# Four streams of eight attention layers on one core: the steps of every engine in a new order

## The chip, the core and the metric

One core of a Trainium2 chip runs the whole program. Its engines each work through a queue of their own: TensorE (PE; its weight loads are shown apart as PEld), VectorE (DVE), ScalarE (ACT), GpSimd (POOL) and SyncE (SP), which here issues the DMAs. The metric is the device time of the program in microseconds, as a median of several runs. "Span" is the time from the first to the last instruction of one profiled execution.

## What is computed

64 sequences of 64 tokens with 128 features, and as many of context, go through eight attentions and what stands between them (layer norms, feed-forward blocks, residual sums). The reference, cut to one attention and to what sets the shapes:

```python
x   = normal((64, 64, 128))          # the sequences
ctx = normal((64, 64, 128))          # their context

def attention(q_in, kv_in, Wq, Wk, Wv, heads, key_mask, query_mask, causal):
    Q, K, V = split(q_in @ Wq), split(kv_in @ Wk), split(kv_in @ Wv)
    scores = Q @ K.T / sqrt(dk)      # 64 x 64 for each sequence and head
    scores = where(key_mask, -inf, scores); if causal: scores = where(col > row, -inf, scores)
    return softmax(scores) @ V * query_mask
# layer 0: two attentions of 16 heads, with layer norms and fc1, fc2
# layer 1: one of 16 heads, output projection, feed-forward of 512 with a gate
# layer 2: two of 16 heads (one causal), output projections, feed-forward of 512 with relu
# layer 3: three times: relu on Q, K, V, 4 heads, layer norm by the sample's deviation, leaky block
```

Attentions 0 to 4 have 16 heads (8 pairs), attentions 5 to 7 have 4 heads (2 pairs).

## The kernel before

**Tiling.** Eight sequences form a stream, four streams form a group, and two groups (0 and 1) cover the 64 sequences. A stream's tensors lie as 128 partitions x 512 elements. Every piece of work is a step with a name, and it belongs to a group, an attention (0 to 8, where 8 is the tail behind attention 7) and a stream (0 to 3). `1.4.2` in the tables is group 1, attention 4, stream 2.

**What sets the order.** Nothing is scheduled when the program is built. The dictionary `ORDER` holds a hand-over list for each engine, `walk` reads it, and `step` issues the instructions of one name. Each step waits on semaphores for its operands, and on PE also for the readers of the PSUM bank that it writes. Every engine works strictly through its list, so a step that waits holds up all that is behind it. PSUM has eight banks in four pairs (`pair0` to `pair3`).

**The names on PE.** `x`, `x1`, `q`, `kv`, `o`, `ctx` are transposes of 128x512 (L695). `pq`, `pk`, `up0` to `up3` are single projections (L708); `pv` writes V in 64x64 pieces (L815); `wo`, `fc2` are L702, `down` L782, `ff` L792. `first`, `length`, `ksum`, `maskrow` make the key mask (L826 to L846). Scores are made twice: `A0`, `A1` (bf16, L916, mask terms L911) only to find each row's maximum, and `B0`, `B1` (f32, the same lines), which are exponentiated. `maxrow` (L846) turns the maxima into a row that B adds. `v0` to `v3` multiply probabilities by V (L935; L964 for 4 heads), and `t0`, `t1` turn the result back (L949).

**The names elsewhere.** DVE reduces A (`mx0` to `mx3`, L1363), negates (`nm`, L1343), spreads the rows (`mrow`, `lrow`, L1350), scales the outputs (`O0`, `O1`, L1153 and L1164), and does sums, layer norm statistics (`sum`, `kvstats`, `n3q`: L1085, L1088) and norms (`n1`, `n3`: L1108; `nq`, `nkv`: L1095). ACT exponentiates B (`e0` to `e3`, L1011) and moves PSUM to SBUF (L977). POOL makes reciprocal deviations and some sums.

**Filling requests.** On PE, `name@24` says which banks a step takes, and `+3` behind it asks for three filling requests ahead of it: products of a constant bf16 tile (`warm`, L683) into the banks that the step is about to write. They compute nothing. A request is one product of 128x512, or four or two side by side on parts of the array. The list before has 323 requests at 244 steps, 581 matmuls in all.

**SP.** Its later loads and stores stand in three loops: the four `Xin` of group 1, the four `C` of group 1, the outputs of group 0, then those of group 1.

Of the kernel before, what the change touches and what calls it, by code (L numbers as in the profile page):

```python
# [32 lines left out]
STREAMS = 4  # L33
# [24 lines left out]
        v2@1+1 v3 t1@5; 0.0.3 maskrow@7; 0.0.1 B0@01 B1@20+1; 0.0.2 A1@12+2; 0.0.1 v0@6+1 v1 v2@3+2 v3 t0@6 t1@3+3;
        0.0.2 maxrow@7+2; 0.0.3 A0@02+3; 0.0.2 B0@31+1; 0.1.0 x1@1+1 kv@0; 0.0.3 A1@31; 0.1.0 pk@1+1 pq@0; 0.0.2 B1@23
        v0@1; 0.1.0 first@0+1; 0.1.1 x1@7; 0.0.2 v1; 0.0.3 maxrow@6; 0.0.2 v2@5 v3 t0@4 t1@5; 0.0.3 B0@13+1 B1@02;  # L60
        0.1.0 pv@3 length@2+1; 0.1.1 kv@7; 0.0.3 v0@6+1; 0.1.2 x1@7+1; 0.1.1 pk@2; 0.1.0 maskrow@5; 0.1.1 pq@4; 0.0.3
        v1; 0.1.0 A0@01+1; 0.0.3 t0@6; 0.1.2 kv@7+1; 0.0.3 v2@5 v3; 0.1.0 A1@01; 0.0.3 t1@5; 0.1.2 pk@7+1; 0.1.1
        first@6 pv@7+2; 0.1.2 pq@6; 0.1.0 maxrow@5; 0.1.1 length@4+3; 0.1.0 B0@01+1 B1@23; 0.1.1 maskrow@1; 0.1.2
        first@0; 0.1.0 v0@1; 0.1.1 A0@12; 0.1.0 v1; 0.1.3 x1@0; 0.1.0 t0@1+1; 0.1.3 kv@0+1; 0.1.1 A1@13; 0.1.2 pv@5
        length@4; 0.1.0 v2@1 v3; 0.1.3 pk@0; 0.1.2 maskrow@4; 0.1.1 maxrow@1+3; 0.1.2 A0@13+1; 0.1.3 pq@5+2; 0.1.0
        t1@4; 0.1.1 B0@01+1; 0.1.3 first@7 pv@6+2; 0.1.2 A1@01+1; 0.1.3 length@7; 0.2.0 kv@6; 0.1.1 B1@20 v0@6 v1;
        0.1.3 maskrow@7; 0.1.2 maxrow@5+1; 0.2.0 pk@4; 0.1.1 v2@5; 0.1.3 A0@01; 0.1.1 t0@7+1 v3; 0.2.0 pv@6; 0.1.1
# [1431 lines left out]
```

## Time and profile before

| | us |
|---|---|
| median of three runs | 1085.9 |
| lowest, highest | 1084.7, 1085.9 |
| span of the profiled execution | 1085.1 |
| of it PE busy, of that filling | 1005.6, 113.4 |
| DVE busy | 840.9 |
| ACT busy | 635.8 |
| POOL busy | 320.4 |

The device time of the profiled execution itself is not among the numbers; the three runs lie 0.4 us below to 0.8 us above its span, so the span stands for it.

A busy share here is a union: two instructions of one engine that overlap count once, so groups of lines add up to more than the engine's busy time. A matmul's duration holds its way through the array, and the next one starts earlier than the last one ends. How long a step holds PE is therefore read from start to start in the timeline.

### The profile page before, as it was taken

The page shows a single profiled execution, that of the slowest core. Times are in us where ns is not written, and L with a number is a line of the kernel's source. Part 1 is how long each engine was busy: PE and PEld are TensorE (multiplying, and loading weights), DVE is VectorE, ACT ScalarE, POOL GpSimd, SP SyncE. Part 2 cuts the span into 40 slices and gives each one's busy share as a digit, 9 for nine tenths or more (in the row PEclk, how much of TensorE's full clock was granted, in tenths as well). Part 3 has the DMA queues.
Part 4 walks back from the last instruction along what each step waited for, and adds up shares of the span by engine and source line. Part 5 has one row for each costly group of instructions (what it writes and reads, how often), then busy time and mean ns, then how long its engine had stood idle before and what let it go on. Part 6 is the DMA issues. An engine that isn't in the chain of part 4 may idle for free.

```text
span 1085.1 us, 38818 instructions
## 1 busy us (share of the span) xinstructions
PE 1005.6 (93%) x16923; PEld 725.6 (67%) x16957; DVE 840.9 (77%) x2336; ACT 635.8 (59%) x938; POOL 320.4 (30%) x405
## 2 busy tenths in 40 slices
PE   8889988899999999999999998889999999998996
PEld 5657665576777677767776776556767677677674
DVE  5897999867476756789878899999567774679986
ACT  5346565567777464555645655556777766464652
POOL 4022245511000113346450313553011020336531
PEclk9999999999999999999979999999999999999998
DMA  7000000000000000000010000000000000000001
GB/s 255 3 22 23 2 3 3 2 2 2 3 3 3 12 9 14 11 2 2 2 31 2 3 13 3 2 2 2 3 2 3 3 3 3 1 2 2 2 2 40
DMA packets 13722, 13.60 MB, mean 13 GB/s; under 512 B 617, under 2 KB 13170, under 8 KB 13298
## 3 DMA queue, kind: packets, MB, share of 16 engines
q1 hardware_dynamic: 13554, 11.11, 3.2%
q8 instruction: 136, 2.23, 0.9%
q14 instruction: 32, 0.26, 0.1%
HBM read 9.01 MB, written 2.10 MB: 10 GB/s over the span
## 4 chain that ended last, share of the span: by engine, by line
PE 42%; DVE 28%; ACT 5%; issue 3%; POOL 2%; POOLq 0%; DVEq 0%; ACTq 0%
PE pair L708 8%; DVE mx L1363 7%; PE pair L916 7%; PE pair L911 5%; PE pair L782 4%; PE pair L695 4%; PE pair L935 3%; DVE stats L1085 3%; PE pair L815 2%; DVE Y L1164 2%; ACT PT L1011 2%; PE pair L702 2%; PE pair L683 2%; DVE Y L1108 2%; PE pair L949 2%
## 5 line engine op out<-in xcount | busy, mean ns | idle before, releaser
L1011 ACT ACTIVATE PT<-pair 128x1024 f32<-128x1024 f32 x184 | 180.3, 1029 | 124.8 <-PE pair L916 115.7
L1363 DVE TENSOR_REDUCE mx<-pair 128x16 f32<-128x1024 f32 x184 | 218.4, 1215 | 42.1 <-PE pair L916 41.6
L916 PEld LDWEIGHTS pair<-KQ 32*128 32x128 f32 (+3 forms) x4416 | 170.7, 157 | 37.6 <-DVE mx L1363 3.4
L916 PE MATMUL pair<-KQ 32*128 32x128 f32 (+3 forms) x4416 | 180.0, 254 | 2.4 <-DVE mx L1363 1.0
L708 PE MATMUL pair<-xf,W_all 128*128 128x512 f32 x336 | 177.4, 623 | 3.2 <-ACT xf L977 1.0
L1390 POOL TENSOR_SCALAR ve<-mv 128x4 f32<-128x4 f32 x64 | 17.0, 265 | 503.3 <-DVE mv L1088 432.5
L683 PE MATMUL pair<-warm 128*128 128x512 bf16 (+3 forms) x581 | 113.4, 395 | 17.8 <-DVE Y L1164 7.8
L977 ACT ACTIVATE KQ<-pair,c 128x512 f32<-128x512 f32 x160 | 100.3, 692 | 42.9 <-PE pair L708 42.2
L935 PE MATMUL pair<-PT,V 128*32 128x64 f32 x5120 | 94.2, 221 | 2.2 <-ACT PT L1011 0.7
L977 ACT ACTIVATE V<-pair 64x512 f32<-64x512 f32 x128 | 79.1, 618 | 26.5 <-PE pair L815 24.7
L935 PEld LDWEIGHTS pair<-PT,V 128*32 128x32 f32 x5120 | 78.3, 110 | 22.2 <-issue 8.7
L708 PEld LDWEIGHTS pair<-xf,W_all 128*128 128x128 f32 x336 | 54.9, 191 | 34.5 <-issue 14.7
L977 ACT ACTIVATE xf<-pair 128x512 f32<-128x512 f32 x80 | 47.4, 598 | 50.6 <-PE pair L695 50.0
L977 ACT ACTIVATE T<-pair 128x512 f32<-128x512 f32 x80 | 48.1, 603 | 42.8 <-PE pair L935 42.5
L1085 DVE BATCH_NORM_STATS2 stats<-X 128x6 f32<-128x128 f32 x320 | 69.8, 281 | 3.7 <-POOL X L1414 1.1
L683 PEld LDWEIGHTS pair<-warm 128*128 128x128 bf16 (+3 forms) x581 | 29.1, 97 | 62.4 <-DVE Y L1164 11.5
L1392 POOL TENSOR_TENSOR rstd<-ve,expo 128x4 f32<-128x4 f32 x64 | 66.6, 1041 | 5.3
L1108 DVE SCALAR_TENSOR_TENSOR Y<-X,mv,row 128x128 f32<-128x128 f32 x192 | 60.8, 378 | 0.9
L977 ACT ACTIVATE KQ<-pair,cols 128x512 f32<-128x512 f32 x72 | 49.5, 696 | 19.5 <-PE pair L708 19.5
L782 PE MATMUL pair<-W_all,KQ 128*128 128x128 f32 x512 | 60.5, 277 | 0.3 <-DVE KQ L1308 0.2
L782 PEld LDWEIGHTS pair<-W_all,KQ 128*128 128x128 f32 x512 | 58.5, 192 | 1.4 <-ACT KQ L977 0.6
L1153 DVE RECIPROCAL rd<-pair 128x32 f32<-128x32 f32 (+1 forms) x128 | 37.4, 292 | 26.3 <-PE pair L949 19.6
(122 smaller groups left out, 1824.0 us busy)
## 6 DMA issues: line engine op xcount, KB each, us to landing
W_all<-weights SPq DMA_DIRECT2D x1, 2880.0 KB, 13.7
Xin<-x SPq DMA_DIRECT2D x8, 256.0 KB, 3.6
C<-ctx SPq DMA_DIRECT2D x8, 256.0 KB, 4.1
out<-X SPq DMA_DIRECT2D x8, 256.0 KB, 2.5
row<-rows SPq DMA_DIRECT2D x1, 1024.0 KB, 6.1
c<-const SPq DMA_DIRECT2D x1, 504.0 KB, 5.5
W_all<-weights SPq DMA_DIRECT2D x1, 192.0 KB, 2.9
c<-const SPq DMA_DIRECT2D x1, 80.5 KB, 2.0
```

What stands on the lines that cost most here:

```text
L683: pe.matmul(bank[c, at:at + FILL], warm[r, 0:columns_], warm[r, :].unsqueeze(1).broadcast_to((rows_, FILL // 128, 128)), start=True, stop= ...
L708: pe.matmul(t[:, 0:TOK], W(name), src[:], start=True, stop=True).then_inc(*banks.full(*use))
L782: mm = pe.matmul(t[:, 128 * j:128 * j + 128], hid[s][:, c, 128 * j:128 * j + 128], W(f"d{a - 1}_{c}"), start=c == 0, stop=c == 3)
L911: pe.matmul(banked[u // 2][:, at:at + 512], fixed, spread, start=u not in begun, stop=False, skip_group_check=True)
L916: last[u] = pe.matmul(banked[u // 2][:, at:at + 2 * S], stationary[rows_, seq].rearrange("p r t -> p (r t)"), moving[rows_, seq].rearrange ...
L935: mm = pe.matmul(outputs[s][32 * c:32 * c + WIDE, at:at + S], V8_padded[s][:, first:first + WIDE], p[:, c // 2, b, c % 2, :], start=True, ...
L977: act.activation(dst, src, f, **kw).then_inc(*banks.drain(use, operand, *event))
L1011: act.activation(PT[:, place, :], banks.of("B", a, s, v)[:], ACT.Exp, scale=float((D // (2 * PAIRS[a])) ** -0.5)).then_inc(*banks.drain((" ...
L1085: dve.bn_stats(stats[lane(tag)][:, j, :], src[:, j, :]).then_inc(*vec.mark("stats", *tag))
L1108: dve.scalar_tensor_tensor(out=Y[s][:, j, :], in0=X[s][:, j, :], scalar=mv[i][:, j, 0:1], in1=rowb(name + "_g"), op0=ALU.subtract, op1=ALU ...
L1363: dve.tensor_reduce(dst, banks.of("A", a, s, v)[:].rearrange("p (u m t) -> p u m t", u=2, t=S), AX.X, ALU.max).then_inc(*banks.drain(("A", ...
L1392: g_.tensor_tensor(rstd[i][:], ve[i][:], expo[:, 0, :], ALU.pow).then_inc(*pool.mark("rstd", *tag))
```

## The change

The lists of PE, ACT, DVE and POOL are replaced by others. They hold the same steps, as many as before: 1152 on PE, 776 on ACT, 849 on DVE, 176 on POOL. What differs is the order, the banks that PE's steps take, the slots of the probabilities, and the filling requests: 148 at 57 steps, 226 matmuls. Streams 2 and 3 stand further behind streams 0 and 1 than before. Steps of attention 5 that depend only on the context (`ksum`, `pv`, `maskrow`, and `km`, `lrow` on DVE) and the transposes `ctx` now stand in the stretch of attentions 1 and 2. SP's later loads and stores get a list too; it names the same sixteen in the same order. `outputs` gets a key for each half, since `v2` may now stand ahead of the use of the first half.

The diff, of the tables only their first lines:

```diff
 ORDER = {
     "PE": """
-        0.0.0 x@7+1; 0.0.1 x@6; 0.0.0 pq@7 pk@6; 0.0.3 x@5; 0.0.1 pq@4+1; 0.0.2 x@7; 0.0.1 pk@3 pv@2+1; 0.0.0 pv@6
-        first@7; 0.0.2 pq@3; 0.0.0 length@7; 0.0.3 pq@6+1; 0.0.0 maskrow@7+2; 0.0.3 pk@2; 0.0.0 A0@02; 0.0.1
...
+        pq@3; 0.0.0 maskrow@0; 0.0.3 x@1; 0.0.2 pv@2; 0.0.0 A0@23; 0.0.2 pq@0; 0.0.1 pk@1; 0.0.0 A1@12; 0.0.3 pq@0;
...
+    "SP": """
+        1.0.0 xin; 1.0.1 xin; 1.0.2 xin; 1.0.3 xin; 1.0.0 cin; 1.0.1 cin; 1.0.2 cin; 1.0.3 cin; 0.8.0 out; 0.8.1 out;
+        0.8.2 out; 0.8.3 out; 1.8.0 out; 1.8.1 out; 1.8.2 out; 1.8.3 out
     """,
...
-                for section.group in range(1, GROUPS):
-                    for s in range(STREAMS):
+                def step(name, a, s):
+                    if name == "xin":
                         sp.wait_ge(*vec.at("sum", 1, s, ago=1))
                         sp.dma_start(Xin[s][:], x_g[section.group, s]).then_inc(*x_in[s].mark(by=16))
-                    for s in range(STREAMS):
+                    elif name == "cin":
                         sp.wait_ge(*banks.ready("pk", 5, s, ago=1))
                         sp.wait_ge(*banks.ready("pv", 5, s, ago=1))
                         sp.dma_start(C[s][:], c_g[section.group, s]).then_inc(*c_in[s].mark(by=16))
-                for section.group in range(GROUPS):
-                    for s in range(STREAMS):
+                    elif name == "out":
                         sp.wait_ge(*(vec if section.group == GROUPS - 1 else pool).at("enc", 8, s))
                         sp.dma_start(o_g[section.group, s], X[s][:]).then_inc(*x_out[s].mark(by=16))
+
+                walk("SP", step)
...
-                        outputs[s] = room("OT", a, s, v // 2)
+                        outputs[s, v // 2] = room("OT", a, s, v // 2)
```

On PE, in group 0 between attentions 1 and 2. `X3`, `Y3` and the like are the tiles of stream 3; `warm` rows are filling requests. Before:

```order
L683 MATMUL pair0<-warm 128x512
L695 MATMUL pair0<-c32,X3 128x128 x4
L683 MATMUL pair0<-warm 128x512
L702 MATMUL pair0<-W_all,kf0 128x128 x4
L683 MATMUL pair0<-warm 128x512
L708 MATMUL pair0<-xf3,W_all 128x512
L683 MATMUL pair3<-warm 128x512
L846 MATMUL pair3<-c16,nm81 128x64
L683 MATMUL pair3<-warm 128x512 x3
L695 MATMUL pair3<-c32,C0 128x128 x4
```

After, in the same stretch (L707 is what L695 was, L720 what L708 was, L961 what L949 was, L858 what L846 was, L850 what L838 was, L822 and L827 what L810 and L815 were):

```order
L961 MATMUL pair3<-c32,T20 128x128 x4
L707 MATMUL pair3<-c32,Y21 128x128 x4
L707 MATMUL pair0<-c32,Y20 128x128 x4
L707 MATMUL pair0<-c32,C1 128x128 x4
L707 MATMUL pair3<-c32,C0 128x128 x4
L850 MATMUL pair1<-kz1,c16 128x8
L850 MATMUL pair1<-kz0,c16 128x8
L720 MATMUL pair0<-kf0,W_all 128x512
L827 MATMUL pair3<-W_all,kf0 64x64 x16
L707 MATMUL pair0<-c32,Y22 128x128 x4
L858 MATMUL pair2<-c16,nm81 128x64
```

The filling has gone from between the steps, and the transposes of the context (`C0`, `C1`) with attention 5's key sums (`kz0`, `kz1`) have come forward.

On DVE, attention 5's mask work (`lm2`, `lrow`, `kms`). Before, it stands in attention 5 of its stream, among the reductions of attention 4:

```order
L1128 TENSOR_REDUCE am0<-X0 128x4
L1131 TENSOR_SCALAR qm0<-am0 128x4
L1363 TENSOR_REDUCE mx3<-pair1 128x2x8
L1363 TENSOR_REDUCE mx3<-pair0 128x2x8
L1363 TENSOR_REDUCE mx3<-pair2 128x2x8
L1335 TENSOR_SCALAR lm20<-pair1 64x8x2 x2
L1343 TENSOR_SCALAR nm83<-mx3 64x64 x2
L1350 TENSOR_TENSOR lrow0<-pair0,c32 32x512
L1355 TENSOR_TENSOR kms0<-pair0,c32 32x128
```

After, it stands in attention 2 (L1347 is what L1335 was, L1375 what L1363 was):

```order
L1120 SCALAR_TENSOR_TENSOR Y1<-X1,mv1,row 128x128 x4
L1347 TENSOR_SCALAR lm20<-pair1 64x8x2 x2
L1347 TENSOR_SCALAR lm21<-pair1 64x8x2 x2
L1347 TENSOR_SCALAR lm23<-pair3 64x8x2 x2
L1347 TENSOR_SCALAR lm22<-pair2 64x8x2 x2
L1375 TENSOR_REDUCE mx3<-pair0 128x2x8
L1375 TENSOR_REDUCE mx3<-pair1 128x2x8
L1097 BN_STATS stats1<-X1 128x6 x4
L1100 BN_AGGR mv1<-stats1 128x2 x4
L1362 TENSOR_TENSOR lrow1<-pair3,c32 32x512
L1367 TENSOR_TENSOR kms1<-pair3,c32 32x128
L1362 TENSOR_TENSOR lrow0<-pair3,c32 32x512
```

All four streams' mask work is now done there, ahead of attention 3.

## Rows read from the trace of the kernel before

**Rows 1.** The page's part on busy time (us, share of the span, instructions).

```profile
span 1085.1 us, 38818 instructions
PE 1005.6 (93%) x16923; PEld 725.6 (67%) x16957; DVE 840.9 (77%) x2336; ACT 635.8 (59%) x938; POOL 320.4 (30%) x405
```

**Rows 2.** Seven stretches: length, each engine's busy time, granted clock, DMA share, GB/s.

```profile
27.00:217.00 190.00, 167.73 (x3448) 116.96 (x3444) 169.04 (x493) 102.27 (x145) 59.28 (x68) 0.97 0.03 8
217.00:461.00 244.00, 237.13 (x3933) 172.71 (x3940) 161.87 (x410) 155.04 (x229) 44.23 (x53) 1.00 0.02 7
461.00:650.00 189.00, 181.31 (x2877) 133.50 (x2889) 158.42 (x443) 106.45 (x160) 72.07 (x80) 0.96 0.03 8
650.00:759.00 109.00, 95.69 (x1735) 65.57 (x1730) 104.34 (x319) 62.94 (x92) 49.31 (x56) 1.00 0.01 2
759.00:1030.00 271.00, 258.51 (x4284) 191.15 (x4295) 192.12 (x519) 172.99 (x256) 66.40 (x80) 1.00 0.01 2
```

**Rows 3.** The same stretches for L683 alone, the filling (PE, PEld busy).

```profile
27.00:217.00 190.00, 35.54 (x203) 8.96 (x203) 0.97 0.03 8
217.00:461.00 244.00, 18.61 (x84) 4.77 (x84) 1.00 0.02 7
650.00:759.00 109.00, 21.63 (x128) 5.80 (x128) 1.00 0.01 2
```

**Rows 4.** Timeline of PE: start, us, line, tiles, count.

```profile
229.33 1.06 PE L916 MATMUL pair<-KQ 32*128 32x128 f32 x32
230.22 0.39 PE L911 MATMUL pair<-mrow,c 32*128 32x512 bf16 x4
...
231.72 0.40 PE L683 MATMUL pair<-warm 128*32 128x512 bf16 x4
231.94 0.62 PE L935 MATMUL pair<-PT,V 128*32 128x64 f32 x32
...
233.46 0.38 PE L683 MATMUL pair<-warm 128*128 128x512 bf16 x1
233.67 1.02 PE L708 MATMUL pair<-xf,W_all 128*128 128x512 f32 x2
```

**Rows 5.** DVE's costliest groups by shape: busy, mean ns of one, idle before.

```profile
L1363 DVE TENSOR_REDUCE mx<-pair 128x16 f32<-128x1024 f32 x184 | 218.4, 1215 | 42.1 <-PE pair L916 41.6
L1085 DVE BATCH_NORM_STATS2 stats<-X 128x6 f32<-128x128 f32 x320 | 69.8, 281 | 3.7 <-POOL X L1414 1.1
L1108 DVE SCALAR_TENSOR_TENSOR Y<-X,mv,row 128x128 f32<-128x128 f32 x192 | 60.8, 378 | 0.9
```

**Rows 6.** Who PE waited for: us in total, times, longest.

```profile
PE pair L683 <- DVE Y L1164: 7.8, 7, 2.9
PE pair L846 <- DVE nm L1343: 6.6, 9, 2.1
PE pair L911 <- DVE mrow L1350: 5.3, 7, 1.7
PE pair L949 <- ACT T L977: 4.1, 10, 0.8
...
PE pair L911 <- DVE mx L1363: 1.3, 5, 0.3
```

**Rows 7.** Short stretches around two falls of the granted clock.

```profile
45.00:48.00 3.00, 0.94 (x21) 0.56 (x9) 2.62 (x6) 0.60 (x1) 0.00 (x0) 1.00 0.04 8
48.00:51.00 3.00, 2.67 (x36) 1.79 (x40) 2.86 (x14) 0.00 (x0) 0.00 (x0) 0.51 0.00 0
...
548.00:551.00 3.00, 1.48 (x7) 0.61 (x9) 2.57 (x5) 1.75 (x4) 2.27 (x2) 0.81 0.00 0
554.00:557.00 3.00, 3.00 (x16) 2.91 (x14) 1.94 (x6) 1.66 (x3) 2.69 (x4) 0.50 0.00 0
```

**Rows 8.** Whom SP waited for.

```profile
SPq L658 <- PE pair L815: 332.4, 4, 272.0
```

**Rows 9.** The whole core: span and mean granted clock.

```profile
core 0: 1085.1 us, clock 0.986
```

More of the change, by code:

```diff
@@ L58 @@
[L58 to L67, printed above, removed]
@@ L168 @@
[L168 to L172 removed]
+        0.0.0 x@0; 0.0.1 x@1+6; 0.0.0 pq@0 pk@1 pv@2; 0.0.1 pv@0; 0.0.0 first@1+2; 0.0.2 x@2; 0.0.0 length@1; 0.0.1
@@ new lines @@
+        ctx@1; 0.3.0 ctx@7; 0.5.1 ksum@2; 0.5.0 ksum@3; 0.2.0 pk@0 pv@7; 0.1.2 kv@1; 0.1.1 maxrow@4; 0.5.1 pv@5; 0.5.0
+        pv@0; 0.1.2 pk@1 pv@4 first@1; 0.1.1 B0@23; 0.1.3 x1@0 kv@4; 0.1.1 v0@5 v1; 0.1.2 length@1; 0.1.3 pk@4 pv@5;
+        0.2.0 x1@0; 0.1.2 maskrow@4; 0.1.1 B1@30 t0@5; 0.1.2 A0@02; 0.1.1 v2@6 v3; 0.2.1 pk@7; 0.1.1 t1@6; 0.1.2
+        A1@20; 0.2.1 pv@7; 0.1.3 pq@6; 0.2.0 fc1@0; 0.2.2 kv@1; 0.3.2 ctx@7; 0.1.2 maxrow@4; 0.5.2 ksum@5; 0.5.3
+        ksum@6; 0.2.0 fc2@0; 0.5.2 pv@1+1; 0.1.3 first@7; 0.2.1 x1@1+2 fc1@1; 0.1.3 length@0; 0.2.1 fc2@7+3; 0.1.3
@@ new lines @@
+        maskrow@3+2; 1.0.3 A0@03; 1.1.1 pk@2; 1.0.3 A1@23; 1.1.0 A0@13; 1.1.1 pv@4 first@5; 1.0.2 B1@13 v0@0; 1.0.3
+        maxrow@1; 1.1.1 length@4; 1.0.2 v1; 1.1.0 A1@32; 1.0.2 t0@0; 1.1.1 maskrow@1; 1.0.2 v2@2 v3; 1.2.0 kv@0; 1.0.2
+        t1@2; 1.3.0 ctx@3; 1.0.3 B0@23; 1.5.0 pv@0; 1.1.1 A0@13; 1.1.0 maxrow@1; 1.0.3 v0@4 v1; 1.5.0 ksum@5; 1.0.3
+        B1@13 t0@4; 1.1.0 B0@03; 1.0.3 v2@2 v3; 1.1.0 v0@4+1 B1@01; 1.0.3 t1@6; 1.1.0 v1; 1.1.2 kv@7 x1@2; 1.2.0 pk@3;
+        1.1.2 pq@4; 1.1.0 t0@6 v2@2 v3; 1.1.2 pk@7 pv@2; 1.1.0 t1@4; 1.1.1 A1@03; 1.1.2 first@4; 1.1.3 x1@2; 1.2.1
@@ new lines @@
+        kv@3; 1.2.0 pv@0; 1.1.1 maxrow@1; 1.1.3 pq@2; 1.3.1 ctx@3; 1.1.1 B0@30; 1.1.2 length@4; 1.1.3 kv@2; 1.1.1
+        v0@6; 1.1.2 maskrow@4; 1.1.1 v1; 1.1.3 pk@2; 1.1.1 B1@03 t0@3; 1.1.3 first@4; 1.2.1 pk@2; 1.1.1 v2@0 v3; 1.1.3
+        length@1 pv@4; 1.1.2 A0@13; 1.1.3 maskrow@5; 1.1.1 t1@0; 1.2.0 x1@4; 1.2.2 kv@1; 1.2.0 fc1@4; 1.1.2 A1@13;
+        1.2.1 pv@0; 1.2.0 fc2@1; 1.3.2 ctx@4; 1.2.3 kv@0; 1.3.3 ctx@4; 1.5.1 ksum@6; 1.5.0 maskrow@7; 1.5.2 pv@0;
+        1.5.3 pv@4; 1.5.1 pv@0; 1.1.3 A0@12; 1.1.2 maxrow@0; 1.2.1 x1@1 fc1@1; 1.1.3 A1@21; 1.2.1 fc2@1; 1.5.2 ksum@0;
@@ L173 @@
+        1.7.1 B0@2; 1.7.2 ksum@1 x@2 maskrow@3+1; 1.7.1 v0@0+1 v1@1; 1.7.2 pq@2 pk@0; 1.7.3 ksum@3 x@4; 1.7.2 pv@5
+        A0@0; 1.7.3 pq@2 pk@3 maskrow@0; 1.7.2 maxrow@1; 1.7.3 pv@4; 1.7.2 B0@3; 1.7.3 A0@0; 1.8.1 x1@2; 1.7.2 v0@3
+        v1@4; 1.8.1 ff@2; 1.7.3 maxrow@5 B0@0+3 v0@3+5 v1@0; 1.8.2 x1@0+6 ff@0; 1.8.3 x1@1+2 ff@1
     """,
     "ACT": """
[L175 to L176 removed]
```

508 lines of the change are left out of this document (254 added, 254 removed).

## The prediction

> **What bounds the kernel now.** I read the busy shares first, then busy time by stretches, then the filling alone, then the timeline of PE. PE is busy for 1005.6 of 1085.1 us and DVE for 840.9 [rows 1], but 113.4 us of PE is filling (the table above), so its own work is 892 us. The stretches show two regimes. In 217 to 461 us PE is busy for 237.1 of 244 us, with 18.6 of filling, while DVE is busy for 161.9: PE bounds [rows 2, 3]. In 27 to 217 us (attentions 0 to 2 of group 0) DVE is busy for 169.0 of 190 us, and in 650 to 759 us, the same place in group 1, for 104.3 of 109; there PE's own work is 167.7 - 35.5 = 132.2 and 95.7 - 21.6 = 74.1 us [rows 2, 3]. DVE bounds there, and PE waits or fills. 461 to 650 and 759 to 1030 us are mixed, PE ahead.
>
> How long a step holds PE is read from start to start. A half of the f32 scores with its row terms holds it for some 1.2 us (0.89 from 229.33 to 230.22, and the row terms ahead of it), and one filling request for 0.22 us: 231.72 to 231.94 for four products side by side, 233.46 to 233.67 for one wide one [rows 4]. So the 323 requests hold PE for 323 x 0.22 = 71 us, less than the 113.4 us of their durations.
>
> **Fewer requests.** 148 are left, 33 us; 175 x 0.22 = 38.5 us of PE time goes. Whether it comes back depends on the bound. I cut PE's list into twenty parts of equal own work (867 us by start to start, 43.4 each; part 0 is the first) and counted. Parts 1 to 3 and 11 to 13, the DVE-bound ones, had 161 requests and have 37. Parts 4 to 10 and 14 to 18, where PE bounds, had 102 and have 59. The first and the last part had 60 and have 52. In the DVE-bound parts the 124 that go (27 us) turn into waiting, since what is late there is DVE. In the PE-bound parts the 43 that go, 9.5 us, come back where the operand was there anyway. In 217 to 461 us PE was idle for only 6.9 us [rows 2], so it seldom still waited behind its filling. I take 8 us, with bounds of 0 and 38.5.
>
> **The balance of DVE against PE.** A step of one engine costs the same wherever it stands; what changes is which steps share a stretch. For each part I added the DVE durations that become due in it (10 to 14 reductions `mx` in each of parts 1 to 3 and 11 to 13 at 1.215, statistics at 0.281, norms at 0.378 [rows 5], and the rest alike). Added singly they come to 961 us, where the busy union is 840.9, so I scale by 0.875. The heaviest parts fall: part 2 from 65 to 59 us, part 12 from 70 to 56. Their neighbours rise: part 1 from 47 to 52, part 3 from 43 to 51, part 13 from 37 to 51. Taking in each part the longer of PE, DVE and ACT, the twenty sum to 948 us before and 938 after: 10 us less, nearly all in group 1. So the further lag of streams 2 and 3 evens a peak but does not turn DVE-bound parts into PE-bound ones. The sum explains 948 of 1085 us; the other 137 are filling on the path and waits within the parts. Bounds: 0 (DVE was not the last in the peak) and 15.
>
> **Distances between a step and what it waits for.** In PE's list I measured the own work between a producer and its consumer, to see where a wait becomes shorter. Longer at the lower quarter or median: `v3` to `t1` from 0.5 to 1.2 us, `pq` to `A0` from 4.2 to 5.7 (median), `A1` to `maxrow` from 3.3 to 4.0, `wo` to the next `q` from 6.6 to 7.8 (median). Shorter: `B0` to `v0` from 2.9 to 2.1 (median), `x1` to `ff` from 1.0 to 0.6, `length` to `maskrow` from 2.3 to 1.1 (median). The waits that the longer ones touch are `maxrow` for `nm`, 6.6 us, the row terms for `mrow`, 5.3, and `t` for ACT, 4.1 [rows 6]. I take 6 us off; bounds are 16 off (all three) and 6 on.
>
> **Banks.** The new list takes banks back sooner. Between the step that fills a score bank and the one that takes it next, the lower quarter of the 368 `mx` cases had 2.3 us of PE work and has 1.8; over all steps, cases under 1.5 us rise from 309 to 382. A reader like `mx` needs 1.215 us [rows 5] once the bank is full, and PE's queue stands still meanwhile with all four streams behind it. Waits of this kind show little before: 1.3 us for `mx` at L911 [rows 6], but 7.8 us of waits for the outputs `Y` stand ahead of filling, which takes its step's bank. I take 4 us on: of the 73 new short cases, those outside the DVE-bound parts, about 40, at 0.1 us each. Bounds are 0 and 73 x 0.5 = 36.
>
> **Edits at nothing.** SP's list names the same sixteen transfers in the same order, and SP spends hundreds of microseconds waiting, 332.4 us at one line [rows 8]; that slack covers them. The moved `pv`, `ctx` and `ksum` of attention 5 are eight sets of about 1.3 + 0.5 + 0.1 us on PE, 15 us that go from PE-bound parts to parts where PE has room; their `km` and `lrow` on DVE (about 1.3 us a stream) go the wrong way. Both are in the part sums. `C` is free for group 1's load no later than before, as `pk` of attention 5, which stays, releases it.
>
> **Clock.** The mean granted clock is 0.986 [rows 9]. It fell from 2.4 to 1.2 GHz behind 3 us in which PE was busy for 0.94 us, and again behind 1.48 of 3 [rows 7]. Without filling PE would be busy for 132 of 190 us in the first DVE-bound stretch, far above those two cases on average, but waits will be longer in places. I take 0 and bound it at 15 us, which is a doubling of the some 30 us at the lower level ((1 - 0.986) x 2 x 1085) at half their length each.
> The Trainium skill (TensorE: Matmul & The Clock Gate, "The HAM clock gate") says that the throttled clock is the default and that sustained activity releases it, which speaks against taking filling out. The falls in the trace agree, and by that rule some of the 38.5 us would be given back, which is the third rival below.
>
> **The sum.** -8 (requests) -10 (balance) -6 (distances) +4 (banks) = -20 us. The span of 1085.1 stands 0.8 us under the median of 1085.9, so the forecast is **1066 us**, 1.8% less.
>
> **Rivals.** First, much faster: the lists fit so well that filling in the DVE-bound parts was itself on the path, as a late PE step makes DVE late. For it: DVE was still idle for 21 of 190 us there [rows 2]. Then 27 us of requests come back too, and the distances give their 16: 1085.9 - 8 - 27 - 10 - 16 + 4 = 1029 us.
> Second, slower: banks decide. If the 73 new short reuses each cost the 0.5 us by which one falls short of `mx`, the sum is -24 + 36 = +12 us, **1098 us**. It beats the gains from about 50 such waits on. For it: one queue, eight banks, and more own work in each microsecond. Against it: before, PE stood idle for 79 us in all, and most reuses stood well clear of their readers.
> Third, no change: the clock. PE idles longer in the DVE-bound parts, the falls double (+15 us) and the banks cost a little more: about 1084 us.
>
> **How the numbers follow.** Chances: forecast (1050 to 1081) 0.42, much faster 0.20, no change 0.10, slower 0.28, the last above the evidence for banks alone since 1152 steps in a new order leave room for waits that distances do not show. A comparison can tell about 0.2%, 2 us, from nothing. Faster is 0.42 + 0.20 = 0.62, same 0.10, slower 0.28. The range reaches from 1033 us, just above the first rival, to 1102, beyond the second, and leaves out about a tenth on each side.
>
> **What would show it.** The filling busy time should fall from 113.4 to about 52 us (226 matmuls). In the PE-bound stretches PE should stay over 95% busy with hardly any filling, and both should be shorter than now. In attentions 0 to 2 DVE should be 90% busy or more and PE idle should grow. If banks decide, `mx` and the outputs `Y` lead the waits of PE, at far more than 8 us. If the clock decides, the mean granted clock is under 0.97. The prediction is wrong at its root if the DVE-bound stretches shorten by more than 20 us, or if PE idles for over 10% in attentions 3 and 4.

## The result, and the profile after

The changed kernel takes 1098.28 us (median of 7 runs, 1089.12 to 1100.13) against 1085.9 (7 runs): ratio 1.0098, 95% interval 1.0080 to 1.0116. It is 12.4 us slower by the medians (10.6 by the ratio, which goes by means), where 20 us less was forecast. The profiled execution of after has a span of 1097.4 us. Its part on busy time:

```profile
span 1097.4 us, 38302 instructions
PE 987.4 (90%) x16602; PEld 717.4 (65%) x16602; DVE 855.7 (78%) x2336; ACT 643.7 (59%) x938; POOL 321.0 (29%) x405
```

Against [rows 1], PE is busy for 18.2 us less (1005.6 before), but the span is 12.3 us longer: idle PE time grew from 79.5 to 110.0 us. DVE is busy for 14.8 us more with the same 2336 instructions. The stretches of [rows 2], in the same columns:

```profile
27.00:217.00 190.00, 162.31 (x3389) 116.62 (x3388) 165.83 (x476) 105.91 (x152) 53.16 (x61) 0.95 0.03 8
217.00:461.00 244.00, 230.30 (x3793) 169.00 (x3794) 173.81 (x432) 157.45 (x229) 54.11 (x64) 0.98 0.02 7
461.00:650.00 189.00, 176.05 (x2843) 128.30 (x2841) 159.00 (x457) 105.14 (x155) 69.95 (x81) 0.97 0.03 8
650.00:759.00 109.00, 89.42 (x1710) 66.35 (x1710) 93.85 (x274) 63.23 (x93) 41.32 (x46) 0.92 0.01 2
759.00:1030.00 271.00, 258.70 (x4154) 189.14 (x4155) 195.43 (x515) 173.94 (x254) 66.93 (x78) 1.00 0.01 2
```

and the filling alone (L695 now) in two of them, as [rows 3]:

```profile
27.00:217.00 190.00, 9.00 (x45) 2.39 (x45) 0.95 0.03 8
650.00:759.00 109.00, 1.21 (x4) 0.31 (x4) 0.92 0.01 2
```

Two things are to be seen. DVE doesn't fill the stretches that it was to bound: 165.8 of 190 us and 93.9 of 109, where it had 104.3 of 109 before. And the granted clock (the column behind the busy times) is lower in three of the five: 0.95, 0.98 and 0.92 where before has 0.97, 1.00 and 1.00. (The same stretch of time does not hold quite the same steps in both.) Over the whole core it is 0.968 against 0.986 [rows 9]. PE's waits, as [rows 6] (us in total, times, longest); the row left out is the wait for the first loads:

```profile
PE pair L923 <- DVE mx L1375: 10.1, 11, 1.6
PE pair L923 <- ACT PT L1023: 9.4, 14, 2.1
PE pair L707 <- DVE Y L1107: 6.2, 4, 2.5
PE pair L707 <- DVE X L1127: 4.9, 2, 2.8
PE pair L720 <- ACT xf L989: 4.8, 8, 1.0
...
PE pair L695 <- DVE Y L1176: 3.1, 3, 1.3
PE pair L923 <- DVE Y L1176: 3.0, 2, 2.7
PE pair L928 <- DVE mx L1375: 3.0, 4, 2.0
PE pair L923 <- DVE mrow L1362: 2.8, 5, 0.9
```

L923 writes the row terms, the first products into a score bank; `mx` (DVE) and `PT` (ACT) are the readers of the score banks. These two are waits for a bank, and neither led before. Summed over all rows of that view, from before to after: `nm`, `mrow` and `T`, the operands that the new distances were to help, fall from 7.0 + 7.2 + 4.8 to 1.1 + 3.2 + 2.2 us, 12.5 less. `mx` and `PT` rise from 4.6 + 5.9 to 15.1 + 17.0, 21.6 more (of the waits for `PT`, 1.5 and 2.7 us are those of `v` for its operand, not for a bank). `Y`, `X` and `xf` rise from 13.1 + 2.2 + 1.0 to 18.6 + 6.0 + 7.1, 15.4 more. Within `Y` it is the norm (L1107, before L1095) that rises, from 2.6 to 7.7; the attention's outputs `Y` (L1176, before L1164) stay at 10.3 and 9.9. So these 15.4 us are mostly ends of normalisation chains and the moves `xf` to SBUF, not banks. (A wait for several semaphores stands under the last.)

### The profile page after: what moved, and what is told of

The parts are those of the page before. It is cut to its first block, busy times and chain, and to the rows that moved or that the text cites. A ratio compares the mean times of both kernels' runs of the same rounds, so it can differ in the third digit from the quotient of the medians.

```text
span 1097.4 us, 38302 instructions
## 1 busy us (share of the span) xinstructions
PE 987.4 (90%) x16602; PEld 717.4 (65%) x16602; DVE 855.7 (78%) x2336; ACT 643.7 (59%) x938; POOL 321.0 (29%) x405
## 4 chain that ended last, share of the span: by engine, by line
PE 64%; DVE 27%; ACT 4%; issue 3%; POOL 1%; DMA 0%; SPq 0%; POOLq 0%; ACTq 0%; DVEq 0%
PE pair L720 13%; PE pair L928 11%; PE pair L923 8%; PE pair L947 7%; DVE mx L1375 6%; PE pair L707 5%; PE pair L794 5%; PE pair L827 3%; PE pair L961 3%; DVE stats L1097 2%; PE pair L714 2%; ACT PT L1023 2%; PE pair L838 2%; DVE rq L1169 2%; DVE Y L1176 2%
## 5 line engine op out<-in xcount | busy, mean ns | idle before, releaser
L1023 ACT ACTIVATE PT<-pair 128x1024 f32<-128x1024 f32 x184 | 182.9, 1023 | 160.5 <-PE pair L928 152.5
L1375 DVE TENSOR_REDUCE mx<-pair 128x16 f32<-128x1024 f32 x184 | 219.9, 1218 | 45.4 <-PE pair L928 44.0
L928 PEld LDWEIGHTS pair<-KQ 32*128 32x128 f32 (+3 forms) x4416 | 175.5, 163 | 42.0 <-issue 6.7
L928 PE MATMUL pair<-KQ 32*128 32x128 f32 (+3 forms) x4416 | 185.4, 260 | 5.4 <-DVE mx L1375 3.0
L720 PE MATMUL pair<-xf,W_all 128*128 128x512 f32 x336 | 174.8, 625 | 5.6 <-ACT xf L989 4.8
L1402 POOL TENSOR_SCALAR ve<-mv 128x4 f32<-128x4 f32 x64 | 16.9, 264 | 471.4 <-DVE mv L1100 471.4
L947 PEld LDWEIGHTS pair<-PT,V 128*32 128x32 f32 x5120 | 78.5, 111 | 28.4 <-issue 16.2
L720 PEld LDWEIGHTS pair<-xf,W_all 128*128 128x128 f32 x336 | 54.3, 191 | 39.3 <-issue 17.9
L923 PE MATMUL pair<-mrow,c 32*128 32x512 bf16 (+1 forms) x368 | 47.1, 395 | 25.0 <-ACT PT L1023 9.2
L1362 DVE TENSOR_TENSOR mrow<-pair,c 128x512 bf16<-128x512 f32 (+1 forms) x64 | 43.6, 682 | 20.5 <-PE pair L858 20.1
L1299 DVE SCALAR_TENSOR_TENSOR X<-pair,X 128x512 f32<-128x512 f32 x40 | 27.5, 688 | 39.7 <-PE pair L714 21.3
```

What stands on the lines that cost most here:

```text
L720: pe.matmul(t[:, 0:TOK], W(name), src[:], start=True, stop=True).then_inc(*banks.full(*use))
L923: pe.matmul(banked[u // 2][:, at:at + 512], fixed, spread, start=u not in begun, stop=False, skip_group_check=True)
L928: last[u] = pe.matmul(banked[u // 2][:, at:at + 2 * S], stationary[rows_, seq].rearrange("p r t -> p (r t)"), moving[rows_, seq].rearrange ...
L947: mm = pe.matmul(outputs[s, v // 2][32 * c:32 * c + WIDE, at:at + S], V8_padded[s][:, first:first + WIDE], p[:, c // 2, b, c % 2, :], star ...
L1023: act.activation(PT[:, place, :], banks.of("B", a, s, v)[:], ACT.Exp, scale=float((D // (2 * PAIRS[a])) ** -0.5)).then_inc(*banks.drain((" ...
L1362: dve.tensor_tensor(dst[s][0:n, :].rearrange("p (m t) -> p m t", m=8), banks.of(*use)[0:n, 0:S].unsqueeze(1).broadcast_to((n, 8, S)), K32( ...
```

## The experiments

All were timed beside before on the same chip; ratios are to before there (medians 1081.25 to 1087.15 us), with 95% intervals. "Part n" is a twentieth of PE's own work, as in the prediction.

### Order and filling apart

e1: the new order with the old 323 requests at the steps where the old list has them. e2: the old order with the new 148 at their 57 steps. e3 and e4: either order with none. Only the +n in PE's list change; e2 and e3 begin:

```
-        0.0.0 x@7+1; 0.0.1 x@6; 0.0.0 pq@7 pk@6; 0.0.3 x@5; 0.0.1 pq@4+1; ...
+        0.0.0 x@7; 0.0.1 x@6+6; 0.0.0 pq@7 pk@6; 0.0.3 x@5; 0.0.1 pq@4; ...      (e2)
+        0.0.0 x@7; 0.0.1 x@6; 0.0.0 pq@7 pk@6; 0.0.3 x@5; 0.0.1 pq@4; ...        (e3)
```

> The new order with the filling requests of the old one: the same 323 at the same 244 steps, in place of its own 148. Theory CLOCK (the 12 us come from the filling that went, by way of the granted clock and of waits that it had covered): the mean granted clock returns to about 0.985 and the time falls to 1080 to 1088 us. Rival ORDER (the new order waits more in itself): the clock returns too, but the time stays at 1094 us or more, since 175 requests more are 38 us of work on PE and only part of them falls into waits.

Measured: 1131.84 us, 1.0461 (1.0438 to 1.0485).

> The old order with the new filling: 148 requests at the 57 steps at which the new order has them, the other 175 gone. Theory CLOCK: slower than 1085.9 by about 8 to 15 us, with a mean clock of 0.97 or less. Rival ORDER: 1075 to 1086 us, since requests that delayed ready steps in the parts bound by PE are gone (my prediction's term was 8 us), whatever the clock does.

Measured: 1093.19 us, 1.0104 (1.0083 to 1.0125).

> The old order with no filling request at all. Theory CLOCK: clearly slower, 1100 us or more, with the mean clock under 0.95. Rival ORDER: within 10 us of 1085.9, what the lower clock costs being given back by 71 us of PE time that is no longer taken.

Measured: 1079.27 us, 0.9981 (0.9966 to 0.9997).

> The new order with no filling request. Theory CLOCK: 1105 to 1115 us, clock under 0.955. Rival ORDER: within 4 us of 1098, as its 148 requests stand in few bunches where PE waits anyway.

Measured: 1098.65 us, 1.0159 (1.0134 to 1.0184).

Of the two theories ORDER's times hold for e1, e3 and e4 (though e1's clock came back only to 0.974). In e2 it fails: its 1075 to 1086 us were missed, and the time is 12 us above before's there, as CLOCK had it.

Without any filling the new order is 19.4 us slower, more than the whole loss. By the ratios the loss adds up from the runs alone: taking the old filling away -2 us (1.0000 to 0.9981), the new order in place of the old one +19 (0.9981 to 1.0159), its own filling put in -7 (1.0159 to 1.0098), together +10.6. In the old order all 323 requests, 71 us of holding PE, cost 2 us net. Requests put at the other order's steps cost 14 us (e2 over e3) and 33 us (e1 over e4).

The pages of e3 and e4 (spans 1079.5 and 1096.3 us) show where the new order's loss lies:

```profile
PE 956.1 (89%) x16342; PEld 702.3 (65%) x16376; DVE 839.5 (78%) x2336; ACT 635.3 (59%) x938; POOL 322.1 (30%) x405
```

```profile
PE 954.2 (87%) x16340; PEld 704.1 (64%) x16376; DVE 855.1 (78%) x2336; ACT 644.1 (59%) x938; POOL 321.6 (29%) x405
```

PE is busy for as long in both. What grows is its idle time, from 123.4 to 142.1 us. PE's waits in e3, then e4:

```profile
PE pair L859 <- DVE nm L1356: 16.9, 15, 3.4
PE pair L924 <- DVE mrow L1363: 7.7, 10, 1.4
PE pair L962 <- ACT T L990: 7.0, 15, 1.1
...
PE pair L924 <- ACT PT L1024: 4.6, 6, 1.2
...
PE pair L924 <- DVE mx L1376: 2.7, 7, 1.1
```

```profile
PE pair L724 <- DVE Y L1124: 12.8, 6, 4.1
PE pair L940 <- DVE mx L1392: 9.8, 10, 1.6
PE pair L940 <- ACT PT L1040: 9.8, 15, 2.1
PE pair L724 <- DVE X L1144: 8.0, 2, 5.5
...
PE pair L940 <- DVE mrow L1379: 4.6, 5, 1.8
...
PE pair L875 <- DVE nm L1372: 3.2, 3, 1.7
```

The exchange of before and after shows bare: `nm` falls from 16.9 to 3.2 us at its line, and `mx`, `PT` and the chain ends `Y` (L1124 is the norm) and `X` more than take its place.

### Filling fitted to the waits

e5 and e6 give either order as many requests as fitted into the waits for an operand that e3 and e4 showed: 190 at 76 steps, and 166 at 51. From e4 to e6:

```
-        0.0.0 x@0; 0.0.1 x@1; 0.0.0 pq@0 pk@1 pv@2; 0.0.1 pv@0; 0.0.0 first@1; ...
+        0.0.0 x@0; 0.0.1 x@1; 0.0.0 pq@0 pk@1 pv@2; 0.0.1 pv@0; 0.0.0 first@1+7; ...
```

> The old order with 190 filling requests at 76 steps, each as many as fit into the wait for an operand that the same order showed there without any filling (one request for every 0.27 us of a wait over 0.4 us). CLOCK (the time follows how long the granted clock is low, 56 us of the old order's span without filling and 78 us of the new one's, at about half a microsecond lost for each): the requests lie in idle time and keep the clock up, so the time falls under the 1079.3 us without filling, to about 1065. STRUCTURE (the low clock only goes along with the waits, it doesn't make them): a fitted request saves nothing and costs what it overlaps, 1079 to 1090 us.

Measured: 1084.13 us, 0.9997 (0.9969 to 1.0025).

> The new order with 166 filling requests at 51 steps, fitted in the same way to the waits that the new order showed without filling. CLOCK: low clock falls from 78 us to under 40 and the time from 1098.7 us to about 1078, and the distance to the old order with fitted filling shrinks from 19 us to under 8. STRUCTURE: 1095 to 1105 us, the distance stays 15 us or more, whatever the clock shows.

Measured: 1101.64 us, 1.0156 (1.0119 to 1.0193).

Whole core of e3, then of e5:

```profile
core 0: 1079.5 us, clock 0.971
```

```profile
core 0: 1077.5 us, clock 0.986
```

The clock rose and the time didn't fall, so CLOCK as written (half a microsecond gained for each at the upper level, requests free in the waits) is refuted; both runs lie where STRUCTURE had them, and the orders stay 17 us apart. What CLOCK left out is what the requests hold up; the section on why the prediction was wrong puts both together.

### GpSimd's additions of a bias row

e7 and e8 cut all 68 of GpSimd's additions of a bias row to a 128x512 tile to one element, in the old and the new order. The biases are left out of the result; the expectation calls the rows zeros, which they are not.

```
-                    g_.tensor_tensor(X[s][:], X[s][:], rowb(name + "_b").unsqueeze(1).broadcast_to((P, NT, 128)),
+                    g_.tensor_tensor(X[s][:, 0, 0:1], X[s][:, 0, 0:1], rowb(name + "_b")[:, 0:1],
```

> The old order and its own filling, with GpSimd's 68 additions of a bias row to a whole 128x512 tile (1.27 and 1.36 us each, all the rows are zeros) cut to one element a partition. PORT (VectorE's norms are held while such an addition runs, up to 1.43 us for a norm of 0.34 us): VectorE's busy falls by 10 us or so in both orders, more in the new one. The chain behind each norm gets 1.2 us shorter in both, so this run is only the base for the next: 1065 to 1085 us.

Measured: 1059.72 us, 0.9772 (0.9737 to 0.9807).

> The same cut in the new order with its own filling. PORT: the distance between the orders, 12.4 us with the additions, shrinks to under 5 us, and no norm of VectorE takes over 0.8 us. STRUCTURE or CLOCK: the distance stays 10 us or more, though the long norms are gone.

Measured: 1088.08 us, 1.0025 (0.9999 to 1.0051).

The distance grew to 28.4 us instead of shrinking, so PORT isn't why the new order is slower. (The two runs also lie far apart in clock, which is priced in the section on why the prediction was wrong: PE was at the lower level for 7.4 us in e7 and for 64.3 in e8, means of their runs.) But the cost is real: DVE's busy time falls by 26.1 us in the old order (840.9 to 814.8) and by 23.5 in the new (855.7 to 832.2), though none of its own instructions changed. The page of e7:

```profile
PE 994.6 (94%) x16923; PEld 719.8 (68%) x16957; DVE 814.8 (77%) x2336; ACT 635.7 (60%) x938; POOL 247.6 (23%) x405
```

### Spliced orders

e9 to e14 have no filling. Every engine goes by one order up to a point of time in its trace, and by the other for the steps that are left; e12 changes twice. PE's list at the joint, from e4 to e9:

```
-        1.0.1 length@5; 0.7.3 A0@1; 1.0.1 maskrow@4; 0.7.3 maxrow@5; 1.0.1 A0@01 A1@23; 0.7.3 B0@0; 1.0.0 ...
+        1.0.1 length@5; 0.7.3 A0@1; 1.0.1 maskrow@4; 0.7.3 maxrow@7 B0@0 v0@6 v1@3; 0.8.2 x1@6 ff@2; 1.0.2 x@3 ...
```

> No filling. Every engine goes by the new order up to 552 us of its trace (584 of TensorE's steps, just before the second group's attentions start) and from there by the old one. PLACES (the 19 us by which the new order is slower without filling lie where the per-part comparison of the two traces puts them: nothing net before 552 us, 8 us from there to 760 us, 9 us in the last 60 us): this one costs what the old order costs, 1078 to 1082 us, ratio 0.998 to 1.001. EVERYWHERE (the loss is spread, each stretch under the new order costs its share): 1088 us, ratio 1.007.

Measured: 1092.42 us, 1.0060 (1.0040 to 1.0080).

> No filling. The old order up to 546 us (579 of TensorE's steps), then the new one. PLACES: all of the loss is there, 1095 to 1099 us, ratio 1.013 to 1.016. EVERYWHERE: 1088 us, ratio 1.007. SEED (the new order's later part is only bad because of the state in which its own first part leaves the streams and banks): 1079 to 1083 us here, and 1088 or more in the run before.

Measured: 1117.66 us, 1.0269 (1.0242 to 1.0295).

> No filling. The new order up to 798 us of its trace (847 of TensorE's steps: the second group's attentions 0 to 4 are behind it), then the old one. PLACES: keeps the 8 us lost between 552 and 760 us and saves the 9 us of the last 60 us: 1086 to 1091 us, ratio 1.005 to 1.009. If the last 60 us are slow because streams 2 and 3 stand behind streams 0 and 1 and not because of the steps' order there, the old order can't mend it: 1095 us or more.

Measured: 1098.48 us, 1.0108 (1.0092 to 1.0125).

> No filling. The old order up to 260 us (253 of TensorE's steps), the new one to 552 us, then the old one again. The per-part comparison gives the new order 3 to 6 us in the stretch bound by TensorE (parts 4 to 9). PLACES: 1073 to 1077 us, ratio 0.993 to 0.996, faster than both kernels. EVERYWHERE: 1084 us, ratio 1.003.

Measured: 1100.15 us, 1.0119 (1.0104 to 1.0133).

All four are slower than PLACES had them, by 2 us (e11) to 17 us (e12) over the end of its range, by the ratios. By its total alone e9 would fit EVERYWHERE (1.007), and e11 a tail that is slow by the lag (1095 us or more). The parts of PE's list (us more than in e3; start of the part in e3), worked out from one profiled execution of each, show why:

```
part  from     e4    e9   e10   e11   e12   e13   e14
 0-3     0    2.8   3.8  -2.4  -0.2   2.8  -1.1  -2.1
   4   248   -0.9  -0.5   0.0  -0.5   7.5  -0.5   0.0
 5-9   295   -1.8  -1.8   0.0  -1.8  -1.7  -1.9   0.0
  10   543    5.1  12.9  13.0   5.1  11.3   5.1   1.4
  11   595    4.0   1.3   7.6   7.1   1.3   4.0   0.0
  12   645   -6.4  -0.5  -4.1  -4.0   1.6  -6.4   0.1
  13   712    5.2   1.8   5.6   5.4   0.1   5.2   0.8
14-18   766    0.4   1.3   3.5  11.6  -0.3   3.4   6.3
  19  1012    8.7  -1.1  10.0  -1.3  -1.1  -1.5   8.9
```

Outside a joint a part costs what its order costs in it, whatever stood before: parts 5 to 9 give -1.7 to -1.9 wherever the new order runs there, the last part 9 to 10 us wherever the new order runs and -1.1 to -1.5 wherever the old one does. That is PLACES. (Parts 0 to 3, 11 and 12 differ by 3 to 6 us between traces of one order, so smaller differences say nothing.) What the expectations left out is the joint, 7 to 13 us each (part 10 in e9, e10 and e12; part 4 in e12; parts 14 to 17 in e11): there a few steps, 5 to 12 of PE's in e9 to e11, are done that the other order would have done later, and others are missing. So e13 and e14 change over where only 5 or 6 steps over all engines differ, at 964 and 958 us, and swap the tail alone. From e4 to e13:

```
-        1.5.3 down@2; 1.6.1 x1@3; 1.6.0 pk@0; 1.5.3 x@1; 1.6.1 ff@2; 1.6.0 pq@3; 1.5.2 maxrow@0; 1.6.0 ...
+        1.5.3 down@2; 1.6.1 x1@3; 1.6.0 pk@0; 1.5.3 x@1; 1.6.1 ff@2; 1.5.3 pk@3; 1.6.0 pq@2; 1.6.1 x@5; 1.6.0 ...
```

> No filling. The new order up to 964 us (1036 of TensorE's steps), where both orders have done the same steps but for 5 over all engines, then the old one. PLACES (the last stretch is slow by its own order): the 9 to 11 us of the last 60 us come back and the joint costs under 2 us: 1088 to 1091 us, ratio 1.004 to 1.008, against 1.0159 of the whole new order. LAG (the tail is slow because streams 2 and 3 come to it later): 1096 us or more.

Measured: 1092.37 us, 1.0054 (1.0030 to 1.0077).

> No filling. The old order up to 958 us (1035 of TensorE's steps), then the new one: the mirror of the run before. PLACES: the old order's 1079.3 us and the tail's 9 to 11: 1088 to 1091 us, ratio 1.005 to 1.009. LAG: 1079 to 1082 us.

Measured: 1098.31 us, 1.0115 (1.0084 to 1.0146).

The ratio moves from 1.0159 to 1.0054 with the old tail, and from 0.9981 to 1.0115 with the new one: 11 and 15 us. LAG falls; the tail's own order is slow. (e14 lies 7 us above PLACES' range: beside 8.9 us in the last part it has 6.3 more in parts 14 to 18, around the joint.) PE's timeline at the end (start, us, line, tiles; in brackets the idle time before), e3 then e4:

```profile
1060.94 1.18 PE L977 MATMUL pair<-V,PT 128*64 128x66 f32 x32 [1.11 <-ACT PT L1024]
1062.05 0.66 PE L708 MATMUL pair<-c,X 128*128 128x128 f32 x4
...
1063.68 1.05 PE L805 MATMUL pair<-W_all,xf 128*128 128x128 f32 x8
...
1069.59 1.12 PE L708 MATMUL pair<-c,X 128*128 128x128 f32 x4 [2.33 <-DVE X L1128]
...
1071.80 1.91 PE L805 MATMUL pair<-W_all,xf 128*128 128x128 f32 x8
```

```profile
1039.24 0.66 PE L724 MATMUL pair<-c,X 128*128 128x128 f32 x4 [2.84 <-POOL X L1443]
...
1047.17 1.41 PE L724 MATMUL pair<-c,X 128*128 128x128 f32 x8 [2.51 <-DVE X L1144]
...
1076.78 1.15 PE L993 MATMUL pair<-V,PT 128*64 128x66 f32 x32 [1.11 <-ACT PT L1040]
1083.45 1.12 PE L724 MATMUL pair<-c,X 128*128 128x128 f32 x4 [5.52 <-DVE X L1144]
1085.35 0.58 PE L817 MATMUL pair<-split,c 128*128 128x512 bf16 x1 [0.78 <-ACT xf L1006]
1085.73 1.91 PE L821 MATMUL pair<-W_all,xf 128*128 128x128 f32 x8
```

Behind the last attention product the old order still has the feed-forward steps of streams 0, 1 and 2 to do and waits 2.33 us for stream 3's norm; the new one has done those of streams 0 and 1 earlier and waits 5.52 us for stream 2's. From that product to the end it is still only 1 us longer (18.6 us in e3, 19.5 in e4). Most of the last part's 8.7 us is lost ahead of it, where the new order waits 2.84 and 2.51 us for tiles `X` of its streams; in the old order no such wait of over 1 us stands between 1012 and 1061 us. The same eight products take 1.05 us at the upper clock and 1.91 at the lower.

### GpSimd's cost by itself, and a faster version

e15 cuts, in the old order, only the 24 additions on which no chain of norms waits (these biases are left out). e16 also writes a row with one product of PE ahead of each of those steps' own (another row than the one left out). e17 and e18 do it in full, in the old and the new order: the three rows are split once into bf16 parts by GpSimd, added in PSUM, and nothing is left out.

```
+                    pe.matmul(t[:, 0:TOK], K16("ones3"), after_row[:, i, :].unsqueeze(1).broadcast_to((P, NT, 128)),
+                              start=True, stop=False, skip_group_check=True)
...
-                            dve.wait_ge(*pool.at("bias", name, a, s))
...
-                    g_.tensor_tensor(X[s][:], X[s][:], rowb({("wo", 3): "bo2", ("down", 3): "d2_b", ("down", 5): "d4_b"}[
-                        name, a]).unsqueeze(1).broadcast_to((P, NT, 128)), ALU.add
```

> The old order with its filling. Of GpSimd's 68 additions of a bias row only the 24 on which no chain waits (1.36 us each, the rows of the output projection and of the two down projections) are cut to one element, so that these biases are left out of the result. PORT (while GpSimd adds, VectorE's work on tiles in SBUF is held): VectorE's busy falls by 24/68 of the 26 us that all 68 gave, 9 us, and the time by 5 to 9 us (ratio 0.992 to 0.995). CHAIN (the 25 us came from the 1.2 us by which each chain behind a norm got shorter): no change, ratio 0.999 to 1.001.

Measured: 1077.43 us, 0.9905 (0.9879 to 0.9930).

> As the run before, with one product of TensorE more in each of these 24 steps, three rows of ones against a split bias row of 512 columns, written before the step's own products (it takes another bias row than the one left out, so the values differ, the work doesn't). 24 by the 0.22 us of a filling request are 5 us, mostly in stretches that TensorE bounds. PORT: ratio 0.996 to 0.999, a version that would be a little faster than before. CHAIN: 1.003 to 1.005.

Measured: 1077.93 us, 0.9915 (0.9894 to 0.9935).

> The old order, its filling and the whole computation: the 24 bias rows of the output and down projections are split once into three bf16 parts by GpSimd (ten small operations at its first step of attention 1's normalisation) and added by TensorE as one product of 512 columns more in each of the 24 steps; VectorE no longer waits for the addition. PORT as e15 and e16 had it: ratio 0.990 to 0.994, about 1078 us, faster than both kernels. If the splitting holds GpSimd's first chains, up to 3 us of that are lost.

Measured: 1079.48 us, 0.9933 (0.9916 to 0.9950).

> The same in the new order with its own filling. PORT paid alike by both: 1098 less 9 us, ratio 1.001 to 1.005, and 10 us or more over e17. If the new order paid more of it (the 1.43 us norms): ratio 0.994 to 0.998.

Measured: 1107.25 us, 1.0189 (1.0161 to 1.0217).

CHAIN falls: additions that stand on no chain are worth 10 us, and TensorE's 24 products cost next to nothing. e17 is the fastest complete kernel of the study, 0.7% under before. In the new order the same edit did not help, against both expectations: 1.0189 is 10 us over after's 1.0098, and 28 us over e17. Some 2.5 us of it is the collision at the start that the last section shows, and 8.5 us more at the lower clock may be 3 us; the rest is not explained.

## Why the prediction was wrong

**The step that failed.** The forecast was -20 us and +12.4 came, a gap of 32. Two steps of the sum make it up. The first is that the new order by itself saves time: -10 (balance) -6 (distances) +4 (banks) = -12. e3 and e4 show +19 instead, in the profiled executions all of it idle PE time, and of it 6 to 15 us may have come by way of the clock (below). The balance was to come back nearly all in group 1, and there, in parts 11 to 13, after took 11 us more than before. The second is the clock, taken as 0. That the order costs 19 us is shown; how it splits between clock, banks and chain ends is worked out from prices and waits, not tried by itself.

**The clock, taken as 0.** The time at the lower level in a run is 2 x (1 - mean clock) x span. Worked out for each timed run, means (number of runs; before's are from five sets):

```
               old order                  new order
filling        low us  span us            low us  span us
own             22.1   1083.1 (84)         62.9   1094.7 (7)
none            52.6   1077.6 (12)         89.5   1097.1 (5)
fitted          37.5   1081.5 (12)         65.2   1099.0 (6)
no bias adds     7.4   1057.9 (6)          64.3   1086.2 (12)
rows on PE      25.1   1076.9 (6)          71.4   1104.1 (6)
```

Runs of one and the same kernel differ in it too: after took 1089.12 us at clock 0.979 and 1100.13 at 0.970. Within kernels the span grows by 0.31 us for each at the lower level (139 runs of 19 kernels, each against its own mean), over before's 84 runs by 0.42. Single kernels give anything from 0.04 (e6, 6 runs) to 0.47 (e5, 12 runs), and which of the two moves the other is not shown. At 0.31 to 0.42 the 40.8 us more of after are 13 to 17 us, as much as the whole loss of 12.4. The traces allow about that: PE was busy for 26.2 us at the lower level in before and for 56.4 in after, and if this work took twice its time, as the eight products above nearly did, 15 us went that way at most. Between e3 and e4 the same price gives 11 to 15 of the 19.4 us, but there it is too high: PE was busy at the lower level for 49.2 and 61.9 us, 6 us by the same reckoning, its busy time as a whole did not grow, and the two kernels' own runs give 0.23 and 0.16, 6 to 8 us for the 36.9 us between them. That a price within a kernel also holds between kernels is argued, not shown. The prediction bounded the clock at 15 us, which about holds. Its sign, a mean clock under 0.97, came in the profiled execution (0.968); the seven runs' mean is 0.971.
The Trainium skill (TensorE: Matmul & The Clock Gate, "A second HAM failure mode: psum-queue depth-cycling") describes a kernel whose clock oscillates because PE idles a little between groups as it cycles through PSUM banks. The traces agree in part: from before to after, waits for banks and time at the lower level rise together. But the clock falls without them too: from before to e3 the time at the lower level rises by 35 us, while the waits for `mx` and `PT` go only from 10.5 to 14.2 us.

**Fewer requests, -8.** The size stands up, as far as the price of the clock does. In the old order, taking all 71 us of requests away saved 2 us net while the time at the lower level rose from 17.2 us (before in that set) to 52.6, which is 11 to 15 us by the price above; so the holding itself had cost an estimated 13 to 17 us, a fifth of it. A fifth of 38.5 us is 8. What the prediction did not couple to it is that the same requests bought the clock: the new order's own 148, which hold PE for 33 us, make it 7 us faster and not slower (e4 to after, 89.5 to 62.9 us at the lower level). And requests fit one order only (e1, e2).

**Distances, -6.** The named waits fell by more than that: `nm`, `mrow` and `T` by 12.5 us, inside the bound of 16. But it listed shorter distances too (`x1` to `ff`, `B0` to `v0`) and gave them no price in the sum.

**Banks, +4.** Mis-sized: about 20 us more by the profile's waits, inside the bound of 36. All short reuses were counted, but priced by `mx` alone; `PT`, ACT's exponential, which reads the score banks as well, rose as much (5.9 to 17.0) and was not looked at. That these waits lie on the path with their full size was not tried: a run with other bank numbers would tell it.

**Left out of the sum:** the waits for the ends of the chains, `Y`, `X` and `xf`, 15.4 us more. The price was put only on the waits that led in [rows 6]; waits that were short before had no row there.

**The balance of DVE, -10.** The peaks that it was to level didn't come back as time: parts 11, 12 and 13 of after took 9.1 more, 3.0 less and 5.0 more than before's. "A step of one engine costs the same wherever it stands" failed too: DVE is busy for 14.8 us more with the same instructions. The norms' durations alone grow by 10.8 us, as twelve of them take over 1 us beside GpSimd's work where before has one of 0.6 (last section).

**The sum again.** Without any price it is the one from the runs: -2.1 +19.3 -6.6 = +10.6, by the ratios. In the prediction's terms, if one price of 0.31 to 0.42 us for each at the lower level held everywhere, it is -7 to -9 (requests), +13 to +17 (clock) and +8 to +4 (what is left between e3 and e4 behind the clock, in place of -12), +12 to +14 in all. That it meets the measured +12.4 proves little, as before, e3, e4 and after are all in it. The second rival, slower at 1098 us, named the time to the microsecond with banks as the cause. Banks are in it, at about 20 us of waits instead of 36, but the runs don't let them stand as the one cause, so the match is partly luck. Its chance, 0.28, had been set above the evidence for banks for waits that distances don't show, and such waits came. The third rival (the clock, +15 us) had the clock's term right, and reached "no change" only because it stood on the other terms' -20.

**The signs.** Filling fell to 44.5 us (226 products), where 52 was said. In 217 to 461 us PE was busy for 94.4%, just under the 95 asked for. DVE reached 87% and 86% where 90 was asked for. `mx` led the waits, but at 10.1 us, not far above 8, and the outputs `Y` did not rise. The signs of a prediction wrong at its root stayed away, though it was wrong: the DVE-bound parts did not shorten, and in 217 to 461 us PE idled for 5.6%, not 10.

## What to carry to other kernels

When an order or its filling changes, ask of each resource, not only of the waits that the profile lists now: for PSUM banks follow every reader, and for chains the waits that are short because something covers them. Filling is neither free nor wasted: here it cost an estimated fifth of its holding and returned about as much by the clock, and only in the order that it was made for (the same requests cost 14 and 33 us in the other); compare orders without it. Before tuning an order further, look at what GpSimd does beside VectorE: 24 additions moved to TensorE gave 0.7%, when 1152 steps in a new order lost 1.0%.
